# Causal attention core: the transposes of the hyperbolic maxima behind the fourth main unit, and another order of casts, shift sums and third parts

## The reference, cut to what matters

```python
def _sdpa(q, k, v, scale):
    scores = jnp.einsum('bhtd,bhsd->bhts', q, k) * scale + _causal_bias(q.shape[-2], k.shape[-2], q.dtype)
    return jnp.einsum('bhts,bhsd->bhtd', jax.nn.softmax(scores, axis=-1), v)
...
def _hyp_attn(q, k, v, curv):
    eps = 1e-06
    tq = jnp.sqrt(1.0 / curv + jnp.sum(q * q, axis=-1, keepdims=True))
    tk = jnp.sqrt(1.0 / curv + jnp.sum(k * k, axis=-1, keepdims=True))
    inner = jnp.einsum('bhtd,bhsd->bhts', q, k) - tq * jnp.swapaxes(tk, -1, -2)
    arg = jnp.maximum(-curv * inner, 1.0 + 1e-07)
    dis = jnp.sqrt(1.0 / curv) * jnp.arccosh(arg)
    scores = 1.0 / (eps + dis) + _causal_bias(q.shape[-2], k.shape[-2], q.dtype)
    return jnp.einsum('bhts,bhsd->bhtd', jax.nn.softmax(scores, axis=-1), v)
```

## Time and profile before

| | |
|---|---|
| three runs | 4958.24, 4977.92 (median), 4982.76 us |
| profiled execution, its own time | 4974.08 us |
| its span | 4972.4 us |
| granted TensorE clock, mean over the span | 0.88 |
| busy in the span | TensorE 78%, VectorE 69%, ScalarE 42%, GpSimd 12% |

### The profile page before, as it was taken

The page is one execution under the profiler, slowest core; times in us unless marked ns, Lnnn a source line. Parts: engine busy times, 40 slices in busy tenths (PEclk is TensorE's granted clock), DMA queues, the critical chain, the costliest instruction groups (busy, mean ns, idle before and its releaser), DMA issues. The chain is left out here.

```text
span 4972.4 us, 89619 instructions
## 1 busy us (share of the span) xinstructions
PE 3898.1 (78%) x25263; PEld 2472.9 (50%) x25263; DVE 3431.8 (69%) x7462; ACT 2095.3 (42%) x3970; POOL 581.7 (12%) x1014
## 2 busy tenths in 40 slices
PE   6999799800048988857777776888799999799998
PEld 5777588600025555535555554666444444455554
DVE  4555444388967887867777775667677777477777
ACT  1222144476533333336767675233366666011110
POOL 0111100000000000010000000222111111122221
PEclk8999999955569989968888887899799999899999
DMA  2222144488954444444444443777555544211110
GB/s 80 75 73 77 56 172 175 171 242 276 400 213 128 125 129 122 123 89 91 94 94 92 94 93 71 177 194 195 133 123 123 123 121 100 75 51 51 57 54 29
DMA packets 508033, 616.80 MB, mean 124 GB/s; under 512 B 62202, under 2 KB 428509, under 8 KB 507933
## 3 DMA queue, kind: packets, MB, share of 16 engines
q1 hardware_dynamic: 498684, 614.41, 44.3%
q0 software_dynamic: 9248, 1.18, 0.2%
HBM read 345.06 MB, written 269.21 MB: 124 GB/s over the span
## 5 line engine op out<-in xcount | busy, mean ns | idle before, releaser
L1231 PE MATMUL ps<-k_downT,f_o 128*91 128x256 f32 x1152 | 261.2, 386 | 455.2 <-DVE f_o L1139 455.1
L3158 PE MATMUL ps<-m_we,m_xT 128*128 128x512 f32 x1104 | 507.4, 604 | 0.0
L2489 DVE TENSOR_REDUCE e_neg<-ps 128x2 f32<-128x546 f32 x512 | 369.7, 723 | 121.2 <-PE ps L2264 112.1
L1231 PEld LDWEIGHTS ps<-k_downT,f_o 128*91 128x91 f32 x1152 | 183.6, 162 | 524.4 <-issue 456.2
L2426 ACT ACTIVATE e_probT<-ps 128x546 f32<-128x546 f32 x512 | 320.6, 627 | 231.4 <-PE ps L2270 226.8
L3093 DVE SCALAR_TENSOR_TENSOR m_acc<-ps,m_weight,m_acc 128x256 f32<-128x256 f32 x552 | 257.6, 480 | 119.2 <-PE ps L3158 105.4
L3158 PEld LDWEIGHTS ps<-m_we,m_xT 128*128 128x128 f32 x1104 | 203.5, 192 | 212.7 <-issue 195.6
L587 DVE TENSOR_REDUCE b_new<-b_gu 128x1 f32<-128x1638 f32 x64 | 119.0, 1859 | 211.5 <-ACT b_gu L654 211.5
L2264 PE MATMUL ps<-e_k,e_q 96*128 96x273 bf16 x1024 | 213.1, 292 | 28.3 <-POOL e_block_mask L2222 16.1
L654 ACT COPY b_gu<-ps 128x273 f32<-128x273 f32 x384 | 148.5, 387 | 189.0 <-PE ps L692 189.0
L2270 PE MATMUL ps<-e_q,e_k 99*128 99x273 bf16 x1024 | 208.3, 285 | 9.3 <-DMA e_q<-e_shift 1.4
(11 more groups left out here) (375 smaller groups left out, 9040.7 us busy)
## 6 DMA issues: line engine op xcount, KB each, us to landing
s_gate<-b_gu SPq DMA_DIRECT2D x32, 819.0 KB, 4.0
s_up<-b_gu SPq DMA_DIRECT2D x32, 819.0 KB, 3.7
c_g<-s_gate SPq DMA_DIRECT2D x32, 819.0 KB, 7.0
s_gated<-c_g SPq DMA_DIRECT2D x32, 819.0 KB, 8.4
d_g<-s_gated SPq DMA_DIRECT2D x32, 819.0 KB, 10.7
d_u<-s_up SPq DMA_DIRECT2D x32, 819.0 KB, 10.6
s_o<-d_o SPq DMA_DIRECT2D x32, 819.0 KB
f_o<-s_o SPq DMA_DIRECT2D x32, 819.0 KB, 4.6
```

Source lines behind the costliest of these rows:

```text
L1231: last = nc.tensor.matmul(ps[0:R, t // 2, (t % 2) * D:(t % 2 + 1) * D], o[:, u, k, t * R:(t + 1) * R], downT[:, k, :], start=(k == 0), sto ...
L2489: nc.vector.tensor_reduce(neg[:, u, g // 2, :, 4 * (g % 2) + a], ps[:, bank:bank + 2, 0:T], AX.X, ALU.max, negate=True).then_inc(S["looked ...
L3158: last = nc.tensor.matmul(ps[0:R, EBANK[m % 4], :], xT[:, u, k, t * R:(t + 1) * R], we[:, k, 2 * p:2 * p + 2, :].rearrange("p e d -> p (e ...
```

## The change

Four places of the hand-written order change; no instruction is added, removed or altered.

```diff
@@ TensorE
                 emit((MAIN, 2), (PRE, 4), (PRE, 5))
+                emit((MAIN, 3), (PRE, 6), (PRE, 7), (PRE, 8))
                 if mains:
                     turn(now, u, 1, posts)
-                emit((MAIN, 3), (PRE, 6), (PRE, 7), (PRE, 8))
@@ ScalarE
                 if mains:
+                    exponential(now, u, b, 3)
                     first_part_hyp(now, u)
-                    exponential(now, u, b, 3)
+                    exponential(now, u, b, 4)
                     second_part_hyp(now, u)
-                    exponential(now, u, b, 4)
                     exponential(now, u, b, 5)
@@ ScalarE
                     log_of_distance(then, tu, 2)
+                    second_part(then, tu)
                     log_of_distance(then, tu, 3)
-                    log_of_distance(then, tu, 4)
                 if mains:
                     exponential_hyp(now, u, 2)
                 if pres:
-                    second_part(then, tu)
+                    log_of_distance(then, tu, 4)
@@ VectorE
+                if pres:
+                    top_scores(then, tu, b)
                 if mains:
                     remainder_hyp(now, u)
                 if pres:
-                    top_scores(then, tu, b)
                     clamp(then, tu)
+                    largest(then, tu, b, 0)
                 if mains:
                     third_part_hyp(now, u)
                 if posts:
                     divide(post, pu, pi, 3)
                 if pres:
-                    largest(then, tu, b, 0)
                     square(then, tu)
@@ VectorE
                 if mains:
                     add_shift(now, u, b, 2)
+                if mains:
+                    add_shift(now, u, b, 3)
                 if pres:
                     third_part(then, tu)
-                if mains:
-                    add_shift(now, u, b, 3)
```

## The result

The changed kernel takes 4948.95 us in the median of ten runs (4946.32 to 4962.68), the kernel before 4977.81 us (4958.24 to 4994.77, ten runs): a ratio of 0.9944, interval 0.9929 to 0.9959. It is faster by 0.56%, 29 us.

A forecast was written before the change was run, and what follows sets the result against it. The prediction took the causal stage to be bound by a chain between engines; removing idle times of 1.39 and 0.80 us per pass gains 72 us, half clock takes back 17, leaving 55: 4920 us, range 4892 to 4964.

The forecast's parts named there:

- What bounds the kernel: Causal attention: a chain between engines; VectorE's idle 1.39 before `tops` 3 and ScalarE's 0.80 before `exponential_hyp` 3 set the period.
- Transposes behind MAIN 3: TensorE does MAIN 3 and PRE 6 to 8 while formerly parked; VectorE's wait before `tops` 3 goes: 1.39 us per pass.
- Casts and shift sums: `second_part` and `add_shift` 3 move earlier, so ScalarE's idle time before `exponential_hyp` 3 goes: 0.80 us per pass.
- The sum: Period of the causal pass falls from 27.31 to 25.1 us at full clock, 72 us in all.
- What takes part of it back: TensorE's half clock from return transposes to PRE 4, now without slack, hits one pass in three: 17 us lost.
- the stretch that I priced at 1.72: TensorE from the return transposes behind `copy_sum` 2 to PRE 4; half clock there costs 1.72 us per pass hit.
- the one with the half clock in each pass: TensorE at half clock behind `copy_sum` 2 in every pass: period 26.8, gain 21 us, 4953 us; chance 0.10.
- the third rival: The causal period settles at 27.3 us again and only early passes gain, 4 us: 4970 us; chance 0.09.
- the sign named for a wrong forecast: VectorE's square stays at 27 us with a new wait in its loop, or GpSimd's transfers delay TensorE before MAIN 4.
- the wait of 2.2 us that I found nowhere: New wait per causal pass that a period settling at 27.3 us again would need; the prediction saw no source.
- GpSimd's transfers and SyncE's loads: With `third_part` 0.4 us earlier, GpSimd's shift transfers come no later and SyncE's loads keep their order: cost nothing.

The follow-up runs named there:

- e9_before_fill_all: The kernel before the change, with thrown-away matmuls in all four idle times of TensorE: 4963.28 us, ratio 0.9976 to the kernel before.
- e6_fill_all: The changed kernel with thrown-away matmuls of 512 columns in all four idle times of TensorE: 4890.21 us, ratio 0.9837 to the kernel before.
- e8_fill_small: The changed kernel with four thrown-away matmuls of only 16 columns behind PRE 1: 4942.04 us, ratio 0.9938 to the kernel before.

## Why the prediction was wrong

*What bounds the kernel* was right: both idle times were on the loop. At full clock their removal takes the period from 27.2 to 25.0 (`e9_before_fill_all`, `e6_fill_all`).

*Transposes behind MAIN 3* was right. They start without a wait, `tops` 3 follows without a gap, and `remainder_hyp` waits for the cast in none of the 30 passes.

*Casts and shift sums* was right as a step: `third_part` and `exponential_hyp` 3 no longer wait, `raw` 0 comes 0.88 earlier behind `distance` (8.08, where it was 2652.45 - 2643.49 = 8.96), and in the spared pass `tops` 2 starts 0.03 behind the end of PRE 4 (2403.15 + 0.33). That TensorE's stretch is left without slack was foreseen.

*The sum* at full clock was right: 1.39 + 0.80 = 2.19 per pass was forecast, and 27.2 - 25.0 = 2.2 measured. In time it is 72 us forecast; the runs gave 73 between the two filled kernels, and 80 against the kernel before as it stands, whose own half clock is then counted too.

*What takes part of it back* is the step that failed. It said: "I let one pass in three be hit: 30 / 3 x 1.72 = 17 us". The share was a guess from passes of a kernel with another period, and it was far too low: 25 of 30 passes in the profiled execution. The price was too low as well: 1.66 was measured for the stretch that I priced at 1.72, but the burst behind `copy_sum` 0 costs 0.73 more, and that one stood in no term of the sum. It could have been read before. In the pass taken apart, `distance` starts 2643.49 - 2635.19 = 8.30 after the square, only 0.11 more than the 8.19 at full clock; in the early pass, the one of the earlier trace rows, 2314.63 - 2305.71 = 8.92, the same as in the hit pass of after:

```profile
2305.71 1.92 DVE L1951 SCALAR_TENSOR_TENSOR g_hu<-g_hw 128x1698 f32<-128x1698 f32 x1
...
2314.63 1.70 ACT L1823 ACTIVATE g_hw<-g_hw,g_one 128x1698 f32<-128x1698 f32 x1
...
2326.85 0.56 DVE L1918 TENSOR_REDUCE g_top<-ps 128x3 f32<-128x384 f32 x1 [0.79 <-PE ps L1565]
...
2643.49 1.70 ACT L1823 ACTIVATE g_hw<-g_hw,g_one 128x1698 f32<-128x1698 f32 x1
```

Nor had most of the 1.72 fallen on slack in that early pass, as the prediction says: `tops` 2 (2326.85) waited 0.79 there, and the pass took 29.07 (to 2334.78). The median run is 13.7 us shorter than the profiled one; at 2.47 for each hit that is 5 or 6 fewer of 25, so some 19 of 30. This is an estimate, as no median run was traced; the trace of `e8_fill_small`, of 4946.43 us, shows 19.

*The rivals*: the time came out next to the one with the half clock in each pass (4953), to which I gave 0.10, and its mechanism is the nearest. That the number fits so well is partly luck: it counted one stretch in all passes, the runs had two stretches in most. The long passes of the profiled execution are near 27.3 again, as the third rival had it, and the sign named for a wrong forecast came, the square at 27 us with a new wait in its loop; the wait of 2.2 us that I found nowhere is the half clock on both stretches. For the choice between the rivals I had weighed the settled passes of before, which had an idle time of 1.54 and full clock behind it, over the early pass. The Trainium skill, TensorE: Matmul & The Clock Gate, section "HAM oscillation — how this bites in real kernels", tells of a loop in which each burst behind a long wait starts at half clock again. The waits of its example are longer than the 1.63 behind which the trace of after shows it (0.59), so the page by itself would not have settled this choice; behind 3.36 (0.50) the trace agrees.

*GpSimd's transfers and SyncE's loads*: no wait on them appears, as forecast.

## What to carry to other kernels

When a reorder takes the slack from a stretch of TensorE, price that stretch at half clock wherever the engine idles ahead of it, and do not count on its being rare: here most passes paid. Whether it was at full clock in the old loop said little about the new period. Look also at the other bursts that were at half clock on slack. Then close such an idle time, best by moving its releaser forward (one copy on ScalarE, some 40 us here), else by matmuls into a bank that is about to be overwritten (some 55 us for four places). A control with the same instructions and almost no columns tells the clock from the order in one run.

## What the runs showed of the hardware

The period of a pass is about the same in two kernels whose loops differ by 2.2 us at full clock: 27.31 before, 27.2 to 27.6 in most passes after. That is a coincidence of two causes: filled to full clock, the kernel before stays at 27.2, the changed one comes to 25.0. Which idle times bring the half clock is not a matter of their length alone. In the changed kernel the stretch behind 1.53 ran at 1.00, behind 1.63 at 0.59; behind 3.36 the return transposes took 0.90 at half clock, behind 3.21 in the spared pass 0.54. In the kernel with two fillings it came behind 1.11, while 1.85 was followed by half clock in some passes, as shown there, and by full clock in others, as in this row and stretch:

```profile
2489.82 0.54 PE L1671 MATMUL ps<-c_ident,g_oT 128*128 128x128 f32 x3 [1.85 <-ACT g_oT L1804]
...
2489.82:2493.99 4.17, 4.11 (x55) 3.01 (x57) 2.53 (x8) 4.17 (x9) 0.00 (x0) 1.00 1.15 133
```

What decides between the two was not tried.
